# Attention with four PSUM banks for the scores and three for the exponents, and the exponential taken one unit at a time

## The chip, the core and the metric

The kernel runs on one core of a Trainium2 chip. The metric is the device time of one execution in microseconds (us). Five engines work side by side, each through its own instructions in order: PE (TensorE, matrix products; its weight loads are listed apart as PEld), DVE (VectorE), ACT (ScalarE), POOL (GpSimd) and SP (SyncE, which here only issues transfers). They wait for each other through semaphores. PE writes its products into PSUM, of which the kernel has eight banks of 512 fp32 columns.

## The reference

One transformer layer over 8 sequences of 512 tokens and 256 features: attention with 16 heads of 16 features and a bias by relative position, then a mixture of experts, both added to the input.

```
q, k, v = (layernorm(x) @ W.T, split into heads)
scores = einsum('bhqd,bhkd->bhqk', q, k) * SCALING + position_bias
attn = softmax(scores); ctx = einsum('bhqk,bhkd->bhqd', attn, v)
x = x + ctx @ Wo.T
x = x + shared expert + top-2 of 7 routed experts (layernorm(x))
```

## The kernel before

The program has three parts: `project` (q, k, v and the bias tables), `attend` (the attention up to the context) and `finish` (output projection and experts). The change lies in `attend` alone.

`attend` works through 32 items (NI): 4 groups of heads times 8 sequences, each with 4 heads. An item has 8 steps (STEPS). A step is one pair of heads and one block of 128 positions, and has two units, side 0 and side 1, one for each head of the pair. The two sides sit in the two halves of PE's rows (partitions 0 and up, and 64 and up), so that a matmul of side 0 and one of side 1 can run at the same time. Each unit is 128 x 512 numbers, one PSUM bank.

Every unit is computed twice, in two orientations. `scores` (L731) makes q.k for 128 queries by 512 keys in a bank of pS; DVE (`maxima`, L680) adds the bias and takes the row's maximum. `turn` (L684) and POOL's transfers bring the maxima of an item back, as rows of q_st, into the second orientation. `exponents` (L743) makes k.q minus the maximum for 128 keys by 512 queries in a bank of pE: one matmul per side (L757) and then eight narrow ones (L765) that add the bias in a band, alternating between side 0 and side 1. ACT takes the exponential into prob (L711). `values` (L770) multiplies prob by v into pC, and ACT copies pC out once an item (L719).

The order on PE is written out by hand: each turn of `slot` (L783) has `scores` for the step 15 steps ahead (LEAD), `exponents` for the present step, and after every second step `values` for a part of the item before. Two steps with one `values` are called a pair below; the first of its steps is step A, the second step B. The first item has no `values` in its turns. The last 15 steps have no `scores`. The first 15 steps' scores are made ahead, before the first turn.

The waits that the change touches, with their lines:

- pS has three banks. BANK and PLACES (L557, L558) deal units out to them and `held` (L560) gives the unit whose maximum must have been taken before the bank is written again. In plain words a unit waits for the one three places before it (L739). In step B, side 1 has to wait for side 0 of step A.
- pE has four banks, two per step. A step waits once, in front of both sides, for the exponentials of the step two before it (L753). Its last band matmul raises e_mm once (L768), and ACT takes both banks in one instruction of 1024 columns (L711).

Of the kernel before, what the change touches and what calls it, by code (L numbers as in the profile page):

```python
# [525 lines left out]
def attend(nc, mk, g):  # L526
# [8 lines left out]
    with ExitStack() as ctx:  # L535
# [5 lines left out]
        nparts = sb("nparts", [P, KM, HPG, TT], F32R)  # L541
        turned = sb("turned", [P, 2, KM * HPG * TT], F32)
        den_ld, den_inv = sem("den_loaded"), sem("den_inverted")
        pS = ps("pS", [P, 3, S], F32)
        pE = ps("pE", [P, 4, S], F32)
        pC = ps("pC", [P, S], F32)
        s_mm, max_done, split_done, max_turned, max_out, max_ld = (sem(n) for n in (
            "s_mm", "max_done", "split_done", "max_turned", "max_out", "max_loaded"))
# [5 lines left out]
        STEPS = HPG // 2 * TT  # L554
        LEAD = 7

        PLACES = [*range(6), None, *range(6, 14), None, 14, 15]  # L557
        BANK = {unit: k % 3 for k, unit in enumerate(PLACES)}  # L558

        def held(unit):  # L560

            k = PLACES.index(unit) - 3
            while PLACES[k] is None:
                k -= 3
            return PLACES[k] + 1 - (16 if k < 0 else 0)

        def await_stores(engine):

# [4 lines left out]
        with nc.Block() as block:  # L573
            @block.sync
            def _(sp):
                for j in range(HPG):
                    if j == 1:
                        await_stores(sp)
                        loads["step"](sp, 0, 1, True)
                    loads["band"](sp, 0, j)  # L580
                for r in range(2, RING):
                    loads["step"](sp, 0, r, True)

                def store_ctx(quad, r, par):

                    sp.dma_start(ctx_dram[4 * (quad % 2) + r, quad // 2], ctx_sb[:, par]).then_inc(c_out[par], 16)

                def slot(s, u, quad):
                    hg = quad // 2
                    if s >= 2:  # L590
                        sp.wait_ge(evac, s - 1)
                        store_ctx((s - 2) // 4, (u + 2) % 4, u % 2)
                    if quad % 2 == 0 and hg < HG - 1:
                        if hg >= 1:
                            sp.wait_ge(max_done, MAX0 + 16 * 8 * hg)
                            sp.wait_ge(e_mm, STEPS * 8 * hg)
                        loads["near"](sp, hg + 1, u)
                        loads["band"](sp, hg + 1, u)
                    if quad < QUADS - 1:
                        sp.wait_ge(e_mm, STEPS * s + STEPS)  # L600
                        sp.wait_ge(v_ready, s + 1)
                        loads["step"](sp, quad + 1, u, quad % 2 == 1)

                for quad in range(QUADS - 1):
                    for u in range(4):
                        slot(4 * quad + u, u, quad)

                sp.dma_start(g["wo_f"][:], g["woT"].rearrange("(c p) o -> p c o", p=P)).then_inc(g["small_ld"], 16)
                sp.dma_start(g["ga_f"][:], g["gateT"].rearrange("(c p) e -> p c e", p=P)).then_inc(g["small_ld"], 16)
                sp.dma_start(g["eb"][:], g["expert_bias"].rearrange("(e o) -> e o", o=1)).then_inc(g["small_ld"], 16)  # L610
                sp.dma_start(g["b1s"][:], g["b1"]).then_inc(g["small_ld"], 16)
                sp.dma_start(g["b2f"][:], g["b2"]).then_inc(g["small_ld"], 16)
                sp.dma_start(g["b2_low"][:], g["low_rows"]).then_inc(g["small_ld"], 16)
                for par in range(2):
                    sp.dma_start(g["x1"][:, par], g["x_t"][par]).then_inc(g["x_ld"][par], 16)
                for k in range(WS):
                    load_weights(sp, g, k)
                for u in range(4):
                    slot(NI - 4 + u, u, QUADS - 1)
                    if u == 1:  # L620
                        for par in range(2):
                            wait_apart(sp, passed, c_out[par], 16 * (NI // 2 - 2))
                        sp.dma_start(den[:], den_rows(ctx_dram, 2 * DH * S, DW, 0, DH * S)).then_inc(den_ld, 16)
                    if u == 3:
                        wait_apart(sp, passed, den_inv, 1)
                        sp.dma_start(den_rows(rden_dram, S, DW, 0), den[:]).then_inc(rden_out, 16)
                        wait_apart(sp, passed, rden_out, 16)
                        load_context(sp, g, 0)
                for n in (NI - 2, NI - 1):
                    wait_apart(sp, passed, evac, n + 1)  # L630
                    store_ctx(QUADS - 1, n % 4, n % 2)
# [33 lines left out]
            def _(dve):  # L665
                dve.sem_inc(max_done, MAX0)  # L666

                def maxima(m, step):

                    hg = m // 8  # L670
                    pair, t = divmod(step, TT)
                    for side in range(2):
                        j, r = 2 * pair + side, 2 * step + side
                        if m % 8 == 0 and t == 0:
                            dve.wait_ge(near_ld[j], 16 * (hg + 1))
                        unit = 16 * m + r
                        dve.wait_ge(s_mm, unit + 1)
                        dve.wait_ge(max_done, MAX0 + unit - 3)
                        lead = P * t
                        dve.tensor_tensor_reduce(sums[:, r % 4], pS[:, BANK[r]], near[:, hg % 2, j, lead:lead + S], -1.0, BIG,  # L680
                                                 ALU.add, ALU.min,
                                                 nmax[:, j, t:t + 1]).then_inc(max_done, 1)

# [19 lines left out]
            @block.scalar  # L703
            def _(act):
                def slot(n):
                    par = n % 2
                    for step in range(STEPS):
                        if step == 0 and n >= 2:
                            copy_ctx(n - 2)
                        act.wait_ge(e_mm, STEPS * n + step + 1)  # L710
                        act.activation(prob[:, par, 2 * step:2 * step + 2], pE[:, 2 * (step % 2):2 * (step % 2) + 2],  # L711
                                       ACT.Exp).then_inc(exp_done, 1)

                def copy_ctx(n):
                    par = n % 2
                    act.wait_ge(pv_done, PV0 + 4 * n + 4)
                    if n >= 2:
                        act.wait_ge(c_out[par], 16 * (n // 2))
                    act.activation(ctx_sb[:, par], pC[:, ORDER[0]], ACT.Copy).then_inc(evac, 1)  # L719

                for n in range(NI):
                    slot(n)
                copy_ctx(NI - 2)
                copy_ctx(NI - 1)

            @block.tensor
            def _(pe):
# [3 lines left out]
                def scores(m, r, rounds, step):  # L731

                    pair, t = divmod(step, TT)
                    if step == 0:
                        pe.wait_ge(qk_ld[r], 16 * 8 * rounds)
                    for side in range(2):
                        unit = 2 * step + side
                        rows = slice(HALF * side, HALF * side + KQ)
                        pe.wait_ge(max_done, MAX0 + 16 * m + held(unit))  # L739
                        pe.matmul(pS[:, BANK[unit]], q_st[rows, r, pair, P * t:P * t + P], k_st[rows, r, pair],  # L740
                                  start=True, stop=True).then_inc(s_mm, 1)

                def exponents(n, r, step, quad, u, first):  # L743
# [5 lines left out]
                    if step == 0:  # L749
                        pe.wait_ge(far_ld[r], 32 * (quad // 2 + 1))  # L750
                        pe.wait_ge(max_ld, 32 * (n + 1))
                    if not (first and step < 2):
                        pe.wait_ge(exp_done, STEPS * n + step - 1)  # L753
                    bank = 2 * (step % 2)
                    for side in range(2):
                        rows = slice(HALF * side, HALF * side + KS)
                        pe.matmul(pE[:, bank + side], k_st[rows, r, pair, P * t:P * t + P], q_st[rows, r, pair],  # L757
                                  start=True, stop=False, skip_group_check=True)
                    for half in range(2):
                        a, z = band(2 * t + half)  # L760
                        lead = a - band_start(2 * t + half)
                        for part in range(2):
                            for side in range(2):
                                rows = slice(HALF * side, HALF * side + HALF)
                                ins = pe.matmul(pE[:, bank + side, a:z], place[rows, half],  # L765
                                                bandT[rows, (quad // 2) % 2, pair, part, lead:lead + z - a],
                                                start=False, stop=half == 1 and part == 1, skip_group_check=True)
                    ins.then_inc(e_mm, 1)  # L768

                def values(n, par, t, first=False):  # L770

                    if t == 0:
                        pe.wait_ge(exp_done, STEPS * n + STEPS)
                        pe.wait_ge(v_ready, n + 1)
                        if not first:
                            pe.wait_ge(evac, n)
# [510 lines left out]
```

## Time and profile before

| | |
|---|---|
| median of 3 runs | 1020.58 us (1019.04 to 1022.09) |
| the profiled execution | 1021.6 us, its span 1019.8 us |
| PE busy | 966.6 us, 95% of the span |
| DVE busy | 703.4 us, 69% |
| ACT busy | 514.8 us, 50% |
| POOL busy | 109.4 us, 11% |
| exponential, L711, 256 instructions of 1024 columns | 261.3 us, 1025 ns each |
| maxima, L680, 512 instructions of 512 columns | 324.8 us, 686 ns each |

The span is the time between the first and the last instruction of the program; the profiled execution's own time also has what lies around it. A busy PE is not a PE at its peak: matmuls overlap, their ends are modelled, and an engine that is held up in the middle of a stretch of matmuls can still be listed as busy. For PE, the distance between the starts of two instructions tells more than their lengths.

### The profile page before, as it was taken

How to read it: one execution, taken by the hardware profiler on the slowest of the kernel's cores; microseconds unless marked ns; L12 is line 12 of the kernel's file. 1: busy time of each engine (PE TensorE's matmuls, PEld its weight loads, DVE VectorE, ACT ScalarE, POOL GpSimd, SP SyncE). 2: the span in 40 equal slices, each digit the busy share in tenths (PEclk: the TensorE clock that was granted, in tenths of full speed). 3: DMA queues.
4: the chain of work that ended last, by engine and by line, in shares of the span. 5: the costliest groups of instructions: out<-in, count | busy, mean ns of one | idle time of the engine just before them, and what ended most of it. 6: DMA issues, size and time to landing. Idle time of an engine off the chain costs nothing. (4 is left out here: it accounts for less than half of the span.)

```text
span 1019.8 us, 20280 instructions
## 1 busy us (share of the span) xinstructions
PE 966.6 (95%) x7264; PEld 721.1 (71%) x7264; DVE 703.4 (69%) x2048; ACT 514.8 (50%) x680; POOL 109.4 (11%) x245
## 2 busy tenths in 40 slices
PE   5799599999999999999999499999999999999998
PEld 3688266666666666666665388888888798888887
DVE  5575587777787877777781667666666575766664
ACT  2344046666666666666667355444344334434433
POOL 2111021111111111111111100000000000000000
PEclk9899589999999999999999699999999999999999
DMA  4998864334543444333352411101111110101000
GB/s 115 303 342 282 240 136 125 104 95 120 132 115 105 125 136 127 86 94 93 87 156 80 134 42 52 60 25 43 41 42 43 41 41 21 62 1 42 1 22 21
DMA packets 65715, 100.27 MB, mean 98 GB/s; under 512 B 11256, under 2 KB 39440, under 8 KB 65598
## 3 DMA queue, kind: packets, MB, share of 16 engines
q1 hardware_dynamic: 62386, 97.49, 31.8%
q0 software_dynamic: 3072, 1.11, 1.0%
q8 instruction: 51, 0.84, 0.4%
q10 hardware_dynamic: 172, 0.56, 0.2%
q14 instruction: 34, 0.28, 0.1%
HBM read 63.67 MB, written 34.93 MB: 97 GB/s over the span
## 5 line engine op out<-in xcount | busy, mean ns | idle before, releaser
L680 DVE CUSTOM_DVE_ANT_0 sums<-pS,near 128x512 bf16<-128x512 f32 x512 | 324.8, 686 | 91.0 <-PE pS L740 90.7
L711 ACT ACTIVATE prob<-pE 128x1024 f32<-128x1024 f32 x256 | 261.3, 1025 | 173.4 <-PE pE L765 173.0
L1187 PE MATMUL pD<-w2p,h_p 128*128 128x256 f32 x1536 | 203.0, 285 | 1.8 <-DVE x L1037 1.8
L1187 PEld LDWEIGHTS pD<-w2p,h_p 128*128 128x128 f32 x1536 | 191.4, 188 | 11.2 <-DVE x L1037 2.6
L765 PEld LDWEIGHTS pE<-bandT,place 64*128 64x128 f32 x2048 | 183.6, 188 | 16.4
L1169 PE MATMUL pU<-x2T,w1p 128*128 128x512 f32 x768 | 191.7, 399 | 0.0
L1100 ACT ACTIVATE h_f<-pU,b1s 128x512 f32<-128x512 f32 x128 | 88.1, 688 | 191.8 <-PE pU L1169 185.9
L740 PE MATMUL pS<-k_st,q_st 48*128 48x512 f32 x512 | 171.8, 493 | 11.5 <-DVEq L666 7.7
L765 PE MATMUL pE<-bandT,place 64*128 64x244 f32 (+2 forms) x2048 | 181.8, 270 | 0.0
L740 PEld LDWEIGHTS pS<-k_st,q_st 48*128 48x128 f32 x512 | 75.3, 191 | 142.3 <-DVE nmax L680 132.3
L1169 PEld LDWEIGHTS pU<-x2T,w1p 128*128 128x128 f32 x768 | 141.6, 190 | 29.5
L1037 DVE SCALAR_TENSOR_TENSOR x<-pD,combine,x 128x256 f32<-128x256 f32 x256 | 110.8, 478 | 64.0 <-PE pD L1187 62.4
L757 PE MATMUL pE<-q_st,k_st 62*128 62x512 f32 x512 | 142.6, 423 | 0.0
L779 PE MATMUL pC<-prob,v_aug 128*32 128x512 f32 x1024 | 135.7, 604 | 1.0 <-ACT ctx_sb L719 1.0
L1026 DVE TENSOR_TENSOR h_p<-h_f,h_p 128x512 fp32r<-128x512 f32 x128 | 86.8, 690 | 68.0 <-ACT h_p L1103 65.6
L1103 ACT ACTIVATE h_p<-pU,b1s 128x512 fp32r<-128x512 f32 x128 | 87.2, 681 | 0.0
L757 PEld LDWEIGHTS pE<-q_st,k_st 62*128 62x128 f32 x512 | 61.4, 187 | 6.2 <-ACT prob L711 5.0
L472 PE MATMUL pQ<-xT,w_p 128*128 128x512 f32 x192 | 51.3, 420 | 7.8 <-DVE qk L390 5.8
L472 PEld LDWEIGHTS pQ<-xT,w_p 128*128 128x128 f32 x192 | 37.4, 203 | 19.6 <-DVE qk L390 9.9
L214 POOL TENSOR_SCALAR rtmp<-mv 128x4 f32<-128x4 f32 x16 | 5.8, 364 | 422.8 <-DVE mv L946 359.1
L649 POOL DMA_DIRECT2D q_st<-negated_maxima x64 | 34.8, 548 | 83.5 <-DMA negated_maxima<-turned 83.5
L680 DVE DVE_READ_ACCUMULATOR2_ANT nmax<- 128x1 f32 x512 | 42.4, 83 | 0.0
(102 smaller groups left out, 575.4 us busy)
## 6 DMA issues: line engine op xcount, KB each, us to landing
x<-in_x SPq DMA_DIRECT2D x16, 512.0 KB, 4.4
q_parts<-qk SPq DMA_DIRECT2D x16, 512.0 KB, 5.0
k_parts<-qk SPq DMA_DIRECT2D x16, 512.0 KB, 4.6
q_st<-q_parts SPq DMA_DIRECT2D x64, 128.0 KB, 2.8
k_st<-k_parts SPq DMA_DIRECT2D x64, 128.0 KB, 2.9
ctx<-ctx_sb SPq DMA_DIRECT2D x32, 256.0 KB, 2.7
near<-bias_by_distance SPq DMA_DIRECT2D x16, 448.0 KB, 5.7
v_rows<-vs SPq DMA_DIRECT2D x8, 512.0 KB, 3.4
```

The lines of the kernel that those rows point to most:

```text
L472: ins = pe.matmul(pQ[:, m % 2], w_p[:, a, w, c, P * h:P * h + P], xT[:, par, z, c], start=k == 0, stop=k == 5)
L680: dve.tensor_tensor_reduce(sums[:, r % 4], pS[:, BANK[r]], near[:, hg % 2, j, lead:lead + S], -1.0, BIG, ALU.add, ALU.min, nmax[:, j, t:t ...
L711: act.activation(prob[:, par, 2 * step:2 * step + 2], pE[:, 2 * (step % 2):2 * (step % 2) + 2], ACT.Exp).then_inc(exp_done, 1)
L740: pe.matmul(pS[:, BANK[unit]], q_st[rows, r, pair, P * t:P * t + P], k_st[rows, r, pair], start=True, stop=True).then_inc(s_mm, 1)
L757: pe.matmul(pE[:, bank + side], k_st[rows, r, pair, P * t:P * t + P], q_st[rows, r, pair], start=True, stop=False, skip_group_check=True)
L765: ins = pe.matmul(pE[:, bank + side, a:z], place[rows, half], bandT[rows, (quad // 2) % 2, pair, part, lead:lead + z - a], start=False, st ...
L779: ins = pe.matmul(pC[32 * j:32 * j + 32], v_aug[:, par, t, j], prob[:, par, at], start=t == 0, stop=t == TT - 1, skip_group_check=True)
L1037: dve.scalar_tensor_tensor(out=row, in0=pD[:, t // 2, t % 2], scalar=combine[:, par, t, e:e + 1], in1=row, op0=ALU.mult, op1=ALU.add).then ...
L1100: act.activation(h_f[:, e % 2, m], pU[:, e % 2, m], ACT.Gelu, bias=b1s[:, e, m:m + 1])
L1103: act.activation(h_p[:, e % 2, 0, m], pU[:, e % 2, m], ACT.Gelu, bias=b1s[:, e, m:m + 1]).then_inc(s["h_hi"], 1)
L1169: ins = pe.matmul(pU[:, e % 2, m], w1p[:, e, a, c, P * m:P * m + P], x2T[:, par, c, z], start=k == 0, stop=k == 5)
L1187: ins = pe.matmul(pD[:, t2, u], h_p[:, e % 2, a, m, P * t:P * t + P], w2p[:, e, z, m], start=k == 0 and e < NE - 1, stop=k == 5)
```

## The change

pS gets a fourth bank and pE gives one up. Units now go round robin: unit number modulo 4 for pS, modulo 3 for pE, with units counted over all items. PLACES, BANK and `held` go. Each unit of scores waits for the maximum of the unit four before it. In `exponents` each side has a wait of its own, for the exponential of the unit three before it; the wait of side 1 stands between the two matmuls of L757. The last band matmul of each side raises e_mm, so it counts units and not steps, and ACT takes the exponential of 512 columns, one unit at a time. Other waits on e_mm and exp_done are scaled to match.

```diff
-        pS = ps("pS", [P, 3, S], F32)
-        pE = ps("pE", [P, 4, S], F32)
+        pS = ps("pS", [P, 4, S], F32)
+        pE = ps("pE", [P, 3, S], F32)
...
+        PS, PX = 4, 3
...
-                        act.wait_ge(e_mm, STEPS * n + step + 1)
-                        act.activation(prob[:, par, 2 * step:2 * step + 2], pE[:, 2 * (step % 2):2 * (step % 2) + 2],
-                                       ACT.Exp).then_inc(exp_done, 1)
+                        for side in range(2):
+                            unit = 16 * n + 2 * step + side
+                            act.wait_ge(e_mm, unit + 1)
+                            act.activation(prob[:, par, 2 * step + side], pE[:, unit % PX], ACT.Exp).then_inc(exp_done, 1)
...
-                        unit = 2 * step + side
+                        unit = 16 * m + 2 * step + side
                         rows = slice(HALF * side, HALF * side + KQ)
-                        pe.wait_ge(max_done, MAX0 + 16 * m + held(unit))
-                        pe.matmul(pS[:, BANK[unit]], q_st[rows, r, pair, P * t:P * t + P], k_st[rows, r, pair],
+                        pe.wait_ge(max_done, MAX0 + unit + 1 - PS)
+                        pe.matmul(pS[:, unit % PS], q_st[rows, r, pair, P * t:P * t + P], k_st[rows, r, pair],
...
-                    if not (first and step < 2):
-                        pe.wait_ge(exp_done, STEPS * n + step - 1)
-                    bank = 2 * (step % 2)
+                    bank = [(16 * n + 2 * step + side) % PX for side in range(2)]
                     for side in range(2):
                         rows = slice(HALF * side, HALF * side + KS)
-                        pe.matmul(pE[:, bank + side], k_st[rows, r, pair, P * t:P * t + P], q_st[rows, r, pair],
+                        if 16 * n + 2 * step + side >= PX:
+                            pe.wait_ge(exp_done, 16 * n + 2 * step + side + 1 - PX)
+                        pe.matmul(pE[:, bank[side]], k_st[rows, r, pair, P * t:P * t + P], q_st[rows, r, pair],
                                   start=True, stop=False, skip_group_check=True)
...
-                    ins.then_inc(e_mm, 1)
+                                if half == 1 and part == 1:
+                                    ins.then_inc(e_mm, 1)
```

On PE, a pair in the middle of the second item, from before. Names in brackets are the semaphores on which an instruction waits (max_done is raised by DVE, exp_done by ACT):

```order
L740 MATMUL pS<-k_st,q_st 128x512 [waits max_done] x2
L757 MATMUL pE<-q_st,k_st 128x512 [waits exp_done]
L757 MATMUL pE<-q_st,k_st 128x512
L765 MATMUL pE<-bandT,place 128x244 x8
L740 MATMUL pS<-k_st,q_st 128x512 [waits max_done] x2
L757 MATMUL pE<-q_st,k_st 128x512 [waits exp_done]
L757 MATMUL pE<-q_st,k_st 128x512
L765 MATMUL pE<-bandT,place 128x218 x4
L765 MATMUL pE<-bandT,place 128x154 x4
```

And the same pair of the changed kernel, with the `values` that follow it:

```order
L733 MATMUL pS<-k_st,q_st 128x512 [waits max_done] x2
L750 MATMUL pE<-q_st,k_st 128x512 [waits exp_done] x2
L758 MATMUL pE<-bandT,place 128x244 x8
L733 MATMUL pS<-k_st,q_st 128x512 [waits max_done] x2
L750 MATMUL pE<-q_st,k_st 128x512 [waits exp_done] x2
L758 MATMUL pE<-bandT,place 128x218 x4
L758 MATMUL pE<-bandT,place 128x154 x4
L773 MATMUL pC<-prob,v_aug 32x512 x4
```

The matmuls and their order are the same; what moved is the second wait on exp_done, which now stands on side 1's matmul, in front of all band matmuls of the step.

On ACT, the first items, from before and then of the changed kernel:

```order
L711 ACTIVATE prob<-pE 128x1024 [waits e_mm] x16
L719 ACTIVATE ctx_sb<-pC 128x512 [waits pv_done]
L711 ACTIVATE prob<-pE 128x1024 [waits e_mm] x8
L719 ACTIVATE ctx_sb<-pC 128x512 [waits pv_done]
L711 ACTIVATE prob<-pE 128x1024 [waits e_mm] x8
```

```order
L705 ACTIVATE prob<-pE 128x512 [waits e_mm] x32
L712 ACTIVATE ctx_sb<-pC 128x512 [waits pv_done]
L705 ACTIVATE prob<-pE 128x512 [waits e_mm] x16
L712 ACTIVATE ctx_sb<-pC 128x512 [waits pv_done]
L705 ACTIVATE prob<-pE 128x512 [waits e_mm] x16
```

Each exponential of 1024 columns became two of 512 with a wait each; the copies of the context stand where they stood.

## Rows read from the trace of the kernel before

**Rows 1.** Windows: busy time by engine, clock; columns are stretch, PE, PEld, DVE, ACT, POOL.
```profile
111.00:134.00 23.00, 18.95 (x35) 8.46 (x37) 20.25 (x66) 0.00 (x0) 3.40 (x6) 0.50 0.89 195
134.00:144.00 10.00, 9.80 (x94) 8.47 (x90) 8.99 (x30) 7.06 (x7) 2.19 (x4) 0.85 0.43 95
144.00:537.00 393.00, 392.80 (x3724) 246.08 (x3724) 311.14 (x1020) 256.08 (x263) 63.07 (x116) 1.00 0.41 114
537.00:556.00 19.00, 19.00 (x216) 11.52 (x218) 3.19 (x8) 14.87 (x16) 2.17 (x4) 1.00 0.23 79
```

**Rows 2.** Waits between 144 and 537 us: total, times, longest.
```profile
ACT prob L711 <- PE pE L765: 136.6, 231, 1.2
PEld pS L740 <- DVE nmax L680: 118.9, 232, 0.8
```

**Rows 3.** Timeline of PE, one pair: start, length, instruction.
```profile
401.05 0.50 PE L740 MATMUL pS<-k_st,q_st 48*128 48x512 f32 x2
401.39 0.40 PE L757 MATMUL pE<-q_st,k_st 62*128 62x512 f32 x2
401.63 0.60 PE L765 MATMUL pE<-bandT,place 64*128 64x154 f32 x8
402.06 0.77 PE L740 MATMUL pS<-k_st,q_st 48*128 48x512 f32 x2
...
403.45 1.06 PE L779 MATMUL pC<-prob,v_aug 128*32 128x512 f32 x8
```

**Rows 4.** Timeline of PE's weight loads around the wait in that pair.
```profile
402.34 0.18 PEld L740 LDWEIGHTS pS<-k_st,q_st 48*128 48x128 f32 x1 [0.19 <-DVE nmax L680]
402.35 0.29 PEld L757 LDWEIGHTS pE<-q_st,k_st 62*128 62x128 f32 x2
```

**Rows 5.** Timeline of ACT in that pair and the next one.
```profile
401.19 0.60 ACT L719 ACTIVATE ctx_sb<-pC 128x512 f32<-128x512 f32 x1
402.27 1.03 ACT L711 ACTIVATE prob<-pE 128x1024 f32<-128x1024 f32 x1 [0.48 <-PE pE L765]
...
405.69 1.03 ACT L711 ACTIVATE prob<-pE 128x1024 f32<-128x1024 f32 x1 [1.11 <-PE pE L765]
```

**Rows 6.** Timeline of DVE in the same pair.
```profile
401.59 0.69 DVE L680 CUSTOM_DVE_ANT_0 sums<-pS,near 128x512 bf16<-128x512 f32 x1 [0.82 <-PE pS L740]
402.20 0.08 DVE L680 DVE_READ_ACCUMULATOR2_ANT nmax<- 128x1 f32 x1
```

**Rows 7.** Timeline of PE, start and values of the pair after it.
```profile
404.45 0.51 PE L740 MATMUL pS<-k_st,q_st 48*128 48x512 f32 x2
...
406.81 1.07 PE L779 MATMUL pC<-prob,v_aug 128*32 128x512 f32 x8
```

**Rows 8.** Timeline of PE and ACT where no scores are left.
```profile
542.49 0.62 PE L765 MATMUL pE<-bandT,place 64*128 64x244 f32 x8
...
543.04 1.06 PE L779 MATMUL pC<-prob,v_aug 128*32 128x512 f32 x8
...
544.04 0.50 PE L757 MATMUL pE<-q_st,k_st 62*128 62x512 f32 x2
...
545.03 1.94 ACT L711 ACTIVATE prob<-pE 128x1024 f32<-128x1024 f32 x2 [0.64 <-PE pE L765]
545.06 0.57 PE L765 MATMUL pE<-bandT,place 64*128 64x218 f32 x8
...
545.56 1.07 PE L779 MATMUL pC<-prob,v_aug 128*32 128x512 f32 x8
```

**Rows 9.** Timeline of DVE in the scores made ahead.
```profile
116.58 0.69 DVE L680 CUSTOM_DVE_ANT_0 sums<-pS,near 128x512 bf16<-128x512 f32 x1 [0.27 <-PE pS L740]
```

**Rows 10.** The page, part 5: the other ACT operation of 512 columns.
```profile
L1100 ACT ACTIVATE h_f<-pU,b1s 128x512 f32<-128x512 f32 x128 | 88.1, 688 | 191.8 <-PE pU L1169 185.9
```

**Rows 11.** Timeline of ACT and PE at the end of the stage.
```profile
557.01 0.60 ACT L719 ACTIVATE ctx_sb<-pC 128x512 f32<-128x512 f32 x1
...
557.73 0.19 PEld L779 LDWEIGHTS pC<-prob,v_aug 128*32 128x32 f32 x8 [1.86 <-ACT prob L711]
```

More of the change, by code:

```diff
@@ L555, in attend @@
         LEAD = 7
[L557 to L565, printed above, removed]
+        PS, PX = 4, 3
         def await_stores(engine):
@@ L595, in slot @@
                             sp.wait_ge(max_done, MAX0 + 16 * 8 * hg)
-                            sp.wait_ge(e_mm, STEPS * 8 * hg)
+                            sp.wait_ge(e_mm, 16 * 8 * hg)
                         loads["near"](sp, hg + 1, u)
@@ L599, in slot @@
                     if quad < QUADS - 1:
-                        sp.wait_ge(e_mm, STEPS * s + STEPS)
+                        sp.wait_ge(e_mm, 16 * s + 16)
                         sp.wait_ge(v_ready, s + 1)
@@ L679, in maxima @@
                         lead = P * t
-                        dve.tensor_tensor_reduce(sums[:, r % 4], pS[:, BANK[r]], near[:, hg % 2, j, lead:lead + S], -1.0, BIG,
+                        dve.tensor_tensor_reduce(sums[:, r % 4], pS[:, unit % PS], near[:, hg % 2, j, lead:lead + S], -1.0, BIG,
                                                  ALU.add, ALU.min,
@@ L764, in exponents @@
                                 rows = slice(HALF * side, HALF * side + HALF)
-                                ins = pe.matmul(pE[:, bank + side, a:z], place[rows, half],
+                                ins = pe.matmul(pE[:, bank[side], a:z], place[rows, half],
                                                 bandT[rows, (quad // 2) % 2, pair, part, lead:lead + z - a],
                                                 start=False, stop=half == 1 and part == 1, skip_group_check=True)
-                    ins.then_inc(e_mm, 1)
+                                if half == 1 and part == 1:
+                                    ins.then_inc(e_mm, 1)
                 def values(n, par, t, first=False):
                     if t == 0:
-                        pe.wait_ge(exp_done, STEPS * n + STEPS)
+                        pe.wait_ge(exp_done, 16 * n + 16)
                         pe.wait_ge(v_ready, n + 1)
```

## The prediction

> **What bounds the kernel now.** I read the windows first, then the waits, then the timeline of one pair of steps engine by engine, since the first two only say where to look. In the windows the attention from 144 to 537 us has PE busy for 392.80 of 393 us, while DVE has 311.14 and ACT 256.08 [rows 1]. A reader is to see two things: PE leads this stage, and a busy share of 100% cannot tell whether it is held up inside. The waits can. ACT waits for PE's band matmuls 231 times, 136.6 us in all, so it is far from the bound; the weight loads of the scores wait for DVE's maxima 232 times, 118.9 us, which is twice a pair [rows 2]. The 3724 matmuls of that window at 32 a pair (4 of L740, 4 of L757, 16 of L765, 8 of L779, as the trace counts them) are 116.4 pairs, so a pair takes 393 / 116.4 = 3.38 us.
>
> The timeline of one pair says which of the two waits costs something. Step A starts at 401.05, its L757 at 401.39, its bands at 401.63, step B at 402.06, and the values at 403.45; the next pair starts at 404.45 [rows 3, 7]. So step A takes 1.01, step B 1.39 and the values 1.00 us. The wait at the start of a pair costs nothing: PE is still busy with the values before it. The one in step B does cost. Side 0 of the scores starts at 402.06, side 1 has its weights only at 402.34, after a wait for DVE [rows 3, 4]. What holds it is the three banks: side 1 of B needs the maximum of side 0 of A, which DVE starts at 401.59 and has at 402.20 + 0.08 = 402.28 [rows 6]; PE goes on 0.06 later. That gives the price of a hand-over to PE, 0.06 us. The rows also show that PE passes nothing by a wait: L757's weights come at 402.35, right behind the waiting load, though their banks had long been free [rows 4]. I lean on that below.
>
> **The fourth bank of scores.** Side 1 of B now needs side 1's partner two steps back, in the pair before, so its wait ends long before it is asked. Without the wait, step B would run as a matmul of 512 columns does when PE is warm, 401.63 - 401.39 = 0.24 us each for the scores and for L757 [rows 3], and then the bands up to the values, 543.04 - 542.49 = 0.55 us for the wide ones and 545.56 - 545.06 = 0.50 us for the narrow ones [rows 8]. The values would start at 1.01 + 0.24 + 0.24 + 0.55 = 2.04 us after the pair's start, where they now start at 2.40 [rows 3]; in the next pair at about 2.02 where they now start at 406.81 - 404.45 = 2.36 [rows 7]. So up to 0.35 us a pair is there to be won, 41 us over 116 pairs.
>
> **The third bank of exponents.** With three banks, side 1 of a step needs the exponential of side 0 of the step right before it; before, both sides needed only the step before that. This is the same short loop as the one taken away from the scores, with ACT in DVE's place, and it starts later in the step. Side 0's last band matmul stands next to side 1's, so its exponential starts when the exponential of step A starts now: 402.27 - 401.05 = 1.22 us after the pair's start [rows 3, 5], in the next pair 405.69 - 404.45 = 1.24 [rows 5, 7]. No exponential of 512 columns is in the trace. The nearest is ACT's copy of 512 columns out of PSUM, 0.60 us [rows 5], and the Gelu of 512 columns takes 0.69 [rows 10]. I take 0.60, since the exponential of 1024 columns at 1.03 [rows 5] is 0.43 more than the copy for 512 columns more, as it would be if both follow one line; 0.69 is the upper end. Add 0.06 for the hand-over (upper end 557.73 - 557.61 = 0.12, from ACT's copy to the loads of the values [rows 11]). Side 1 of L757 in step B is then let go at 1.22 + 0.60 + 0.06 = 1.88 us. Undisturbed it would go at 1.01 + 0.24 = 1.25 or a little later. Everything behind it waits too: eight band matmuls, the values, and the next pair. From the release a cold start costs 401.39 - 401.05 = 0.34 us up to the first band [rows 3], and the bands 0.55, so the values start at 1.88 + 0.34 + 0.55 = 2.77, against 2.40 now: 0.37 us more. For the next pair 1.90 + 0.34 + 0.50 = 2.74 against 2.36: 0.38 more. The lost 0.35 of the scores is already in these, since the old wait is no longer part of the path. Over 116 pairs: 116 x 0.375 = 43.5 us. A pair becomes about 3.75 us.
>
> In step A the new wait costs nothing: its side 1 needs side 0 of the B before it, whose exponential is done during the 1.00 us of values plus 0.34. The split on ACT itself costs nothing either. Four exponentials at 0.60 and a quarter of a copy make 2.55 us in a pair of 3.75; what hides them is PE. If that cover were gone it would show as ACT busy all through, and it is not near.
>
> **Where no scores are left** nothing stands between the steps to cover ACT. These are the last 8 pairs (216 matmuls at 28 a pair is 7.7 [rows 1]; the first of the 8 has scores in its step A alone). A pair starts at 544.04, its first exponential at 545.03, its values at 545.56 [rows 8], so 0.99 and 1.52 us in. After the change the release comes at 0.99 + 0.66 = 1.65, the values at 1.65 + 0.34 + 0.50 = 2.49: 0.97 more, 8 x 0.97 = 7.8 us.
>
> **The first item** has no values to cover ACT, so each of its steps waits on the last. From a release 0.34 to the bands, 402.27 - 401.63 = 0.64 from there to the exponential [rows 3, 5], 0.66 for it: 1.64 us a step, or 1.53 if side 0, whose tile is free while side 1 waits, runs ahead by one of the four rounds of bands, (402.06 - 401.63) / 4 = 0.11 [rows 3]. Now a step takes 10 us / (94 / 12) = 1.28 [rows 1]. Seven steps at +0.25 to +0.36: I take +2.
>
> **The scores made ahead**, from 111 to 134 us, are DVE's: 20.25 of 23 us busy [rows 1]. Now and then it waits for a bank's matmul, 0.27 us at a time [rows 9]; a fourth bank takes away perhaps four of those: -1.
>
> **Sum.** 43.5 + 7.8 + 2 - 1 = +52. The profiled execution took 1021.6 us (span 1019.8), which gives 1074; it lies 1.0 above the median of the runs, so 1073. The ends of the unknowns: an exponential of 0.69 adds 0.09 x 124 = 11; a hand-over of 0.12 adds 7; if the start after the release is as warm as between two matmuls (0.24 for 0.34), 12 come off.
>
> What a separate increment of e_mm for each side may cost is not in the sum, because the rows show none: the scores' pair carries two increments and DVE starts at 401.59, 0.04 after its end at 401.55 [rows 3, 6]; the bands carry one, and ACT starts at 402.27, 0.04 after their end at 402.23 [rows 3, 5]. The Trainium skill (TensorE: Matmul & The Clock Gate, "The cost: per-tile semaphore tail") says that increments on neighbouring tiles of the array are carried out one after the other, some 26 ns for each. By that rule one more increment a step, at the worst on the path to the exponential of step A, would be an estimated 0.026 x 124 = 3 us more.
>
> **Rivals.**
> - The exponential of one unit comes in time (faster). ACT starts a unit without the other and is through in half the time, so the loop of 0.66 us could be shorter than I think, and the fourth bank's 41 us would be kept: 1021 - 41 - 1 = 979 us. It decides at one place, side 1 of L757 in step B: its release would have to come by 1.25 us after the pair's start to win all, and by 1.88 - 0.37 = 1.51 to lose nothing. For it speaks that ACT has 136.6 us of waits [rows 2]. Against it: the exponential cannot start before 1.22, and 0.03 to 0.29 us is less than any ACT instruction of 512 columns takes here [rows 5, 10]. 4 in 100. Between the two, no change: 2 in 100.
> - The wait is real but half as dear, because PE works off side 0's bands while side 1 waits. That would need matmuls to pass a waiting load, which rows 4 deny; the path through side 1 (0.34 + 0.55) would also stay. With half the price, 0.19 x 124 = 24, it gives about 1045. 4 in 100.
> - The clock. The granted clock was 1.00 from 144 to 556 us and 0.50 from 111 to 134, where PE had 35 matmuls in 23 us [rows 1]. The change puts a stop of about half a us into every pair and a longer one into each of the last 8. Should the clock fall to its lower level, 1.2 GHz, for a tenth of the stage, the parts of a pair that are PE's own (1.01 + 0.89 + 1.00 = 2.90 us) would take about twice as long there: 12 pairs x 2.9 = 35 us more, 1108. Against it, PE still has work in 2.9 of 3.75 us. The Trainium skill (TensorE: Matmul & The Clock Gate, "A second HAM failure mode: psum-queue depth-cycling") tells of a kernel in which PE paused briefly between groups while it went round the PSUM banks, and the clock kept going down and up; the trace before shows the pauses in step B at an unbroken 1.00, which speaks against it here. 4 in 100.
> - The forecast has the remaining 86 in 100.
>
> **How the numbers follow.** Runs of this kernel differ by some 0.3%, and I take that as the least that can be told from no change. The forecast, the half price and the clock make it slower: 0.94. Faster 0.04, same 0.02. Time 1073 us. For the range the forecast's own unknowns give 1061 to 1091 at their ends; both upper ends together are unlikely. I take 1057 to 1088.
>
> **What would show it.** In the waits, the entry of L740's loads for DVE in step B goes; only the harmless one at a pair's start stays. A new one appears, PE's loads of the exponents' matmuls for ACT's exponential, once a pair (about 0.5 us each) and twice in the first item. Step A keeps 1.01 us, step B goes from 1.39 to about 1.76, the values stay at 1.00, a pair is 3.75. The exponential is 0.60 us, and ACT's busy time rises to some 512 x 0.60 = 307 us for it. The stage after 560 us is only shifted. I am wrong if side 1 of step B is let go before 1.5 us into the pair, if the wait falls on another instruction, or if the granted clock in the attention falls below 1.00.

## The result, and where the time went

| | before | changed |
|---|---|---|
| median | 1021.11 us (1019.04 to 1022.09, 4 runs) | 1071.57 us (1070.60 to 1074.86, 4 runs) |
| span of the profiled execution | 1019.8 us | 1068.8 us |

The ratio is 1.050, with a 95% interval of 1.047 to 1.053. The forecast was 1073 us.

I cut both traces at the same events: on PE the first exponents' matmul, the first `values`, the `values` 115 pairs later and the last scores, and then the first instruction of `finish`. Between the 115 pairs and the last scores lies 1.0 us in both, which the table leaves out. Differences are taken before rounding.

| stage | before | changed | difference |
|---|---|---|---|
| up to the first exponents' matmul | 133.4 | 132.9 | -0.5 |
| from there to the first `values` (the first item) | 13.4 | 18.8 | +5.3 |
| 115 pairs | 3.377 each | 3.716 each | +39.0 |
| from the last scores to `finish` | 26.7 | 34.1 | +7.4 |
| `finish` | 456.9 | 454.7 | -2.2 |

These add up to +49.0, as much as the spans differ. The last line is not the change's: nothing in `finish` was touched, and among the kernels below it takes 454.7 to 457.9 us.

The waits of the changed kernel from 144 to 557 us (engine, line, releaser: total, times, longest):

```profile
ACT prob L705 <- PE pE L758: 154.2, 223, 1.1
DVE sums L672 <- PE pS L733: 112.3, 111, 1.3
PEld pS L733 <- DVE nmax L672: 91.4, 109, 0.8
PEld pE L750 <- ACT prob L705: 73.2, 113, 0.7
...
PE pE L750 <- ACT prob L705: 23.7, 111, 0.3
```

This window holds 111 pairs; that of [rows 2] held 116, with 232 waits of the scores' loads for DVE, two a pair. Now these loads (L733) wait 109 times, once a pair: the wait inside the pair is gone, the one at its start (under the `values` of the pair before) stays. In its place the loads of the exponents' matmuls (now L750) wait for ACT, once a pair, 0.65 us each. ACT itself waits more than before, 1.39 us a pair (154.2 / 111) against 1.18 (136.6 / 116). It is not short of time; it is asked too late.

One pair on PE (start, length, instruction), the counterpart of [rows 3, 7]:

```profile
405.36 0.49 PE L733 MATMUL pS<-k_st,q_st 48*128 48x512 f32 x2
405.69 0.40 PE L750 MATMUL pE<-q_st,k_st 62*128 62x512 f32 x2
405.93 0.62 PE L758 MATMUL pE<-bandT,place 64*128 64x244 f32 x8
406.38 0.39 PE L733 MATMUL pS<-k_st,q_st 48*128 48x512 f32 x2
406.61 0.39 PE L750 MATMUL pE<-q_st,k_st 62*128 62x512 f32 x1
407.23 0.50 PE L750 MATMUL pE<-q_st,k_st 62*128 62x512 f32 x1 [0.23 <-ACT prob L705]
407.23 0.90 PE L758 MATMUL pE<-bandT,place 64*128 64x218 f32 x8
408.06 1.06 PE L773 MATMUL pC<-prob,v_aug 128*32 128x512 f32 x8
409.06 0.50 PE L733 MATMUL pS<-k_st,q_st 48*128 48x512 f32 x2
```

ACT in the same pair, and the weight load that waits for it:

```profile
406.58 1.09 ACT L705 ACTIVATE prob<-pE 128x512 f32<-128x512 f32 x2 [1.13 <-PE pE L758]
```
```profile
407.22 0.18 PEld L750 LDWEIGHTS pE<-q_st,k_st 62*128 62x128 f32 x1 [0.65 <-ACT prob L705]
```

Both scores of step B start together at 406.38, where in [rows 3, 4] the second was held up. Then side 0 of L750 goes at 406.61 and side 1 only at 407.23. The exponential starts 1.22 us into the pair, and 0.64 later side 1's load goes: an exponential of 0.59 and a hand-over of 0.05. Note that PE counts as busy to the very start of its [0.23] of idle time: the hole is 0.6 us wide in the starts and 0.2 in the busy time.

### The profile page after: what moved, and what is told of

The parts are those of the page before. It is cut to its first block and busy times, and to the rows that moved or that the text cites. A ratio compares the mean times of both kernels' runs of the same rounds, so it can differ in the third digit from the quotient of the medians.

```text
span 1068.8 us, 20536 instructions
## 1 busy us (share of the span) xinstructions
PE 987.9 (92%) x7264; PEld 715.1 (67%) x7264; DVE 703.4 (66%) x2048; ACT 531.8 (50%) x936; POOL 109.4 (10%) x245
## 5 line engine op out<-in xcount | busy, mean ns | idle before, releaser
L705 ACT ACTIVATE prob<-pE 128x512 f32<-128x512 f32 x512 | 278.0, 594 | 206.1 <-PE pE L758 206.1
L758 PE MATMUL pE<-bandT,place 64*128 64x244 f32 (+2 forms) x2048 | 202.0, 280 | 0.0
L750 PE MATMUL pE<-q_st,k_st 62*128 62x512 f32 x512 | 170.9, 431 | 29.7 <-ACT prob L705 28.5
L1163 PE MATMUL pU<-x2T,w1p 128*128 128x512 f32 x768 | 189.5, 396 | 0.0
L758 PEld LDWEIGHTS pE<-bandT,place 64*128 64x128 f32 x2048 | 178.1, 190 | 10.6
L733 PE MATMUL pS<-k_st,q_st 48*128 48x512 f32 x512 | 130.4, 473 | 10.3 <-DVEq L658 7.8
L750 PEld LDWEIGHTS pE<-q_st,k_st 62*128 62x128 f32 x512 | 74.1, 189 | 93.2 <-ACT prob L705 90.9
L733 PEld LDWEIGHTS pS<-k_st,q_st 48*128 48x128 f32 x512 | 56.6, 195 | 116.9 <-DVE nmax L672 106.7
```

The lines of the kernel that those rows point to most:

```text
L705: act.activation(prob[:, par, 2 * step + side], pE[:, unit % PX], ACT.Exp).then_inc(exp_done, 1)
L733: pe.matmul(pS[:, unit % PS], q_st[rows, r, pair, P * t:P * t + P], k_st[rows, r, pair], start=True, stop=True).then_inc(s_mm, 1)
L750: pe.matmul(pE[:, bank[side]], k_st[rows, r, pair, P * t:P * t + P], q_st[rows, r, pair], start=True, stop=False, skip_group_check=True)
L758: ins = pe.matmul(pE[:, bank[side], a:z], place[rows, half], bandT[rows, (quad // 2) % 2, pair, part, lead:lead + z - a], start=False, sto ...
L1163: ins = pe.matmul(pU[:, e % 2, m], w1p[:, e, a, c, P * m:P * m + P], x2T[:, par, c, z], start=k == 0, stop=k == 5)
```

## The experiments

All times are medians. Each ratio is to runs of the kernel before taken beside that kernel (their medians are 1020.5 to 1021.1 us). A pair and the two stages are read from one trace of each kernel, the pair as above. "First item" is the time from the first exponents' matmul to the first `values`, "last part" from the last scores to `finish`.

| kernel | time, us | ratio to before (95%) | pair | first item | last part |
|---|---|---|---|---|---|
| before | 1021.1 | | 3.377 | 13.4 | 26.7 |
| changed | 1071.6 | 1.050 (1.047 to 1.053) | 3.716 | 18.8 | 34.1 |
| split_only | 1021.2 | 1.000 (0.998 to 1.001) | 3.378 | 13.5 | 26.8 |
| rr3 | 1020.2 | 0.999 (0.998 to 1.000) | 3.377 | 13.4 | 26.7 |
| rr3_swap | 987.2 | 0.966 (0.964 to 0.968) | 3.067 | 18.7 | 26.7 |
| after_swap | 1100.0 | 1.076 (1.074 to 1.078) | 3.972 | 20.3 | 34.1 |
| before_halfmax | 988.5 | 0.968 (0.967 to 0.970) | 3.110 | 12.8 | 26.7 |
| after_halfmax | 1066.7 | 1.047 (1.044 to 1.051) | 3.718 | 16.5 | 34.1 |
| after_halfexp | 1041.3 | 1.021 (1.019 to 1.024) | 3.505 | 14.7 | 32.4 |
| after_side0_first | 1068.0 | 1.046 (1.044 to 1.048) | 3.716 | 14.4 | 34.1 |
| swap_late | 984.0 | 0.964 (0.962 to 0.965) | 3.066 | 13.3 | 26.7 |

### The two harmless parts

split_only is the changed kernel with the banks as before (PLACES, BANK and `held` are back for pS):

```diff
-        pS = ps("pS", [P, 4, S], F32)
-        pE = ps("pE", [P, 3, S], F32)
+        pS = ps("pS", [P, 3, S], F32)
+        pE = ps("pE", [P, 4, S], F32)
...
-        PS, PX = 4, 3
+        PX = 4
```

> The kernel before with one part of the change: the exponential taken one unit of 512 columns at a time, with a wait for each side, but four banks of exponents and three of scores as before. My theory: with four banks side 1 of a step needs the exponential of side 1 two steps back, which is long done, so nothing stalls: 1021 us (1018 to 1024), a pair of steps 3.38 us, no wait of L757's loads for ACT. Rival, the split itself costs (ACT's fixed cost twice, two increments a step): at least 3 us more, and 1070 if the split were the whole cause.

Measured 1021.2 us, 3.378 us a pair. Taking the exponential one unit at a time, with its 512 instructions, its waits and its increments, costs nothing that can be measured.

rr3 is the kernel before with round robin over its three banks of scores (DVE reads the bank `unit % PS` too):

```diff
+        PS = 3
...
-                        unit = 2 * step + side
+                        unit = 16 * m + 2 * step + side
...
-                        pe.wait_ge(max_done, MAX0 + 16 * m + held(unit))
-                        pe.matmul(pS[:, BANK[unit]], q_st[rows, r, pair, P * t:P * t + P], k_st[rows, r, pair],
+                        pe.wait_ge(max_done, MAX0 + unit + 1 - PS)
+                        pe.matmul(pS[:, unit % PS], q_st[rows, r, pair, P * t:P * t + P], k_st[rows, r, pair],
```

> The kernel before with the other small part: the units of scores go round robin over the three banks (unit number modulo 3, counted over all items) instead of by the table PLACES. My theory: in step B side 1 still waits for side 0 of step A, so 1021 us (1018 to 1024) and a pair of 3.38 us. Rival, the table was worth something: some us slower.

Measured 1020.2 us, 3.377 a pair: the table was worth nothing that can be measured against round robin. So the whole loss sits in the number of banks.

### What side 1 waits for

after_halfexp is the changed kernel with half of each exponential left out. ACT fills the columns left out once, before the first item:

```diff
-                            act.activation(prob[:, par, 2 * step + side], pE[:, unit % PX], ACT.Exp).then_inc(exp_done, 1)
+                            act.activation(prob[:, par, 2 * step + side, 0:S // 2], pE[:, unit % PX, 0:S // 2], ACT.Exp).then_inc(exp_done, 1)
...
+                act.wait_ge(near_ld[0], 16)
+                act.wait_ge(s_mm, 17)
+                for k in range(2 * HPG * TT):
+                    act.activation(prob[:, k // 16, k % 16, S // 2:S], near[:, 0, 0, 0:S // 2], ACT.Exp)
```

> The changed kernel with the exponential taken over the first 256 of a unit's 512 columns (the other half of the exponentials is left out; ACT fills those columns of prob once, before the first item). My theory: what PE waits for in step B is side 0's exponential of step A, nearly all of it its own length. From 1025 ns at 1024 columns and 594 at 512 it should be about 380 ns at 256, so the release comes 0.21 us earlier: a pair falls from 3.71 to 3.50, 115 x 0.21 = 24 us, the last 8 pairs 2, the first item 1 to 2: 1044 us (1036 to 1052). Rival, the hand-overs PE to ACT to PE are the cost and not the length: less than 5 us.

Measured 1041.3 us. The exponential's line on the page of the changed kernel, and of this one:

```profile
L705 ACT ACTIVATE prob<-pE 128x512 f32<-128x512 f32 x512 | 278.0, 594 | 206.1 <-PE pE L758 206.1
```
```profile
L705 ACT ACTIVATE prob<-pE 128x256 f32<-128x256 f32 x512 | 168.5, 381 | 242.4 <-PE pE L762 242.4
```

The instruction is 0.213 us shorter, and a pair is 3.716 - 3.505 = 0.211 shorter; the last part loses 1.7 us over its 8 pairs, again 0.21 each. What is taken off that one exponential comes off the pair in full. The first item is another 4.1 us shorter, where the clock was up from 137 us on (in the changed kernel from 148). That ACT is 50% idle does not help it.

after_halfmax is the changed kernel with half of each maximum left out; before_halfmax leaves out the same in the kernel before:

```diff
-                        dve.tensor_tensor_reduce(sums[:, r % 4], pS[:, unit % PS], near[:, hg % 2, j, lead:lead + S], -1.0, BIG,
+                        dve.tensor_tensor_reduce(sums[:, r % 4, 0:S // 2], pS[:, unit % PS, 0:S // 2], near[:, hg % 2, j, lead:lead + S // 2], -1.0, BIG,
```

> The changed kernel with the same half of the maxima left out. My theory: with four banks DVE is off the path in every pair, so nothing is gained there (3.71 us a pair stays); the scores made ahead, DVE's before, may give 3 us: 1068 us (1063 to 1073). Rival, DVE still holds PE in the changed kernel: 20 us or more gained.

> The kernel before, with DVE's maximum taken over the first 256 of a unit's 512 columns (the other half of the work of the maxima is left out). My theory: the price of the three banks of scores is DVE's time between side 0 of step A and side 1 of step B. DVE's instruction falls from 0.69 to some 0.47 us and its spacing from 0.61 to 0.40; side 1 of B is released before it is asked for, a pair falls from 3.38 to 3.05 to 3.07 us, 115 pairs give 36 us, the scores made ahead some 3 more: 982 us (974 to 990). Rival, PE is at its own limit in step B and DVE's wait is only listed: less than 6 us gained, all of it in the scores made ahead.

In the changed kernel the pair stays at 3.718, so DVE is off the path there. The medians differ by 4.9 us; in the two traces the first exponents' matmul comes 2.4 us earlier and the first item is 2.3 us shorter, mostly since its clock rose earlier (see the windows of both below). In the kernel before, the pair falls to 3.110 and the time by 32 us, to 988.5, inside the stated range, though 6 more than the number I gave. A pair of it on PE:

```profile
401.18 0.50 PE L740 MATMUL pS<-k_st,q_st 48*128 48x512 f32 x2
401.52 0.40 PE L757 MATMUL pE<-q_st,k_st 62*128 62x512 f32 x2
401.75 0.62 PE L765 MATMUL pE<-bandT,place 64*128 64x244 f32 x8
402.21 0.50 PE L740 MATMUL pS<-k_st,q_st 48*128 48x512 f32 x2
402.45 0.48 PE L757 MATMUL pE<-q_st,k_st 62*128 62x512 f32 x2
402.69 0.67 PE L765 MATMUL pE<-bandT,place 64*128 64x218 f32 x8
403.28 1.06 PE L779 MATMUL pC<-prob,v_aug 128*32 128x512 f32 x8
```

Step B runs at 0.24 us a matmul as in a pair with no wait. Its scores still take 0.50 and not 0.39 us as in the changed kernel, and the bands to `values` 0.59 where [rows 8] have 0.50. A trace of the wait for DVE is left:

```profile
402.07 0.08 DVE L680 DVE_READ_ACCUMULATOR2_ANT nmax<- 128x1 f32 x1
402.11 0.28 PEld L740 LDWEIGHTS pS<-k_st,q_st 48*128 48x128 f32 x2
```

The maximum of side 0 of step A is done at 402.15. The first of the two loads goes at 402.11; the second ends at 402.39 and lasts 0.18, so it goes at 402.21: some 0.05 behind the maximum, which is the price of a hand-over, and 0.10 behind the first.

### Which work lies inside the loop

after_side0_first is the changed kernel, but in step B side 0's four bands are issued before side 1's matmul and its wait:

```diff
...
+                    if step % 2 == 1:
+                        for side in range(2):
+                            main(side)
+                            for half, part in four:
+                                near_band(side, half, part)
+                    else:
+                        for side in range(2):
+                            main(side)
+                        for half, part in four:
                             for side in range(2):
...
+                                near_band(side, half, part)
```

Here main(side) is the wait and the matmul of L750, near_band one band matmul with its increment.

> The changed kernel, but in odd steps (step B) PE gets side 0's matmul and its four bands first, and only then side 1's matmul with its wait, and its four bands. PE then has work to issue while it waits. My theory: the path runs through side 1 alone (release, its matmul, its four bands, values), so nothing is gained in a pair: 1071 us (1065 to 1076); in the first item side 0's exponential of step B is ready earlier, which may give 1 to 3 us. Rival, half the price is that side 0's bands stand behind the wait: 1045 to 1055.

Measured 1068.0 us. The pair is 3.716 us to the last digit, and the last part too is unchanged:

```profile
402.30 0.39 PE L751 MATMUL pE<-q_st,k_st 62*128 62x512 f32 x1
402.53 0.57 PE L758 MATMUL pE<-bandT,place 64*128 64x218 f32 x4
402.91 0.50 PE L751 MATMUL pE<-q_st,k_st 62*128 62x512 f32 x1
403.25 0.57 PE L758 MATMUL pE<-bandT,place 64*128 64x218 f32 x4
403.75 1.06 PE L786 MATMUL pC<-prob,v_aug 128*32 128x512 f32 x8
```

Side 0's bands now run at 402.53, in the hole. It is filled and not shorter: side 1 starts at 402.91, 1.87 us into the pair that began at 401.04. The rival of half the price falls. The medians differ by 3.6 us, and what is gained is in the first item, 4.3 us in the traces.

rr3_swap and after_swap change one thing in either kernel, the order in step B:

```diff
+                        if step % 2 == 1:
+                            exponents(n, u, step, quad, u, first and u == 0)
                         if not (last and u + ahead > 3):
                             scores(n + ahead, (u + ahead) % 4, quad + 1 + (u + ahead) // 4, other)
-                        exponents(n, u, step, quad, u, first and u == 0)
+                        if step % 2 == 0:
+                            exponents(n, u, step, quad, u, first and u == 0)
```

> As rr3, and in odd steps (step B) the exponents' matmuls come before the scores' and not after them. Banks stay at three for scores and four for exponents. My theory: the loss in step B was the short loop scores of A, maximum by DVE, scores of B; with L757 and the bands of B in between, side 1's bank is free before it is asked for. A pair takes about 3.04 us (0.34 less), 116 pairs give 39 us: 981 us (975 to 992), and L740's waits for DVE inside a pair go. Rival, the number of banks is what counts and the order is not: 1021.

> The changed kernel (four banks for scores, three for exponents) with the same swap in odd steps. My theory: here the short loop runs over the exponents, and the scores of step B were the only work between the bands of A and side 1 of L757 in B. ACT's release stays at about 1.85 us after the pair's start; the scores now come behind it, 0.26 us more in front of the values: a pair of about 3.97 us, 116 x 0.26 = 30 us more, 1101 us (1090 to 1110). Rival, the stall is not a matter of what covers ACT: 1072.

Both lie in their ranges, 987.2 and 1100.0 us (after_swap 1 below its number, rr3_swap 6 above: the pairs took 3.067 and not 3.04 us, which makes 3 us, and the rest lies in the first item, 18.7 us for 13.4 in the trace). The same edit gains 33 us with three banks of scores and four of exponents (against rr3), and costs 28 us with four and three. PE in rr3_swap, one pair:

```profile
400.04 0.50 PE L732 MATMUL pS<-k_st,q_st 48*128 48x512 f32 x2
400.38 0.40 PE L749 MATMUL pE<-q_st,k_st 62*128 62x512 f32 x2
400.61 0.60 PE L757 MATMUL pE<-bandT,place 64*128 64x154 f32 x8
401.05 0.40 PE L749 MATMUL pE<-q_st,k_st 62*128 62x512 f32 x2
401.29 0.61 PE L757 MATMUL pE<-bandT,place 64*128 64x244 f32 x8
401.74 0.39 PE L732 MATMUL pS<-k_st,q_st 48*128 48x512 f32 x2
402.06 1.06 PE L771 MATMUL pC<-prob,v_aug 128*32 128x512 f32 x8
```

The scores of step B are asked for 1.70 us into the pair, both sides at once; in [rows 3, 4] side 1 was let go at 1.29. After_swap has the same order and this step B:

```profile
404.39 0.40 PE L750 MATMUL pE<-q_st,k_st 62*128 62x512 f32 x1
405.24 0.49 PE L750 MATMUL pE<-q_st,k_st 62*128 62x512 f32 x1 [0.45 <-ACT prob L705]
405.24 0.71 PE L758 MATMUL pE<-bandT,place 64*128 64x218 f32 x6
405.75 0.43 PE L733 MATMUL pS<-k_st,q_st 48*128 48x512 f32 x1
405.79 0.35 PE L758 MATMUL pE<-bandT,place 64*128 64x154 f32 x2
405.98 0.43 PE L733 MATMUL pS<-k_st,q_st 48*128 48x512 f32 x1
406.34 1.07 PE L773 MATMUL pC<-prob,v_aug 128*32 128x512 f32 x8
```

Its pair began at 403.37, so side 1 is again let go at 1.87; the hole is 0.85 us wide, since the scores that had covered 0.24 of it now stand behind it.

### The first item, and a version that beats both

swap_late is rr3_swap with the old order in the first item (`step % 2 == 1 and n > 0` in the edit above).

> As rr3_swap (three banks of scores, four of exponents, exponents before scores in step B), but the first item keeps the old order. In rr3_swap the time from the first exponents to the first values was 18.7 us at a granted clock of 0.50, against 13.5 us in the kernel before, where the clock was up to 1.00 for most of it. My theory: the old order keeps PE busier in the first item, the clock rises as it did before, and those 5 us come back while the pairs stay at 3.07 us: 982 us (979 to 986). Rival, the clock of the first item does not follow from its order: 987.

Measured 984.0 us. The clock during the first item (PEclk is the first of the last three numbers), before, changed and swap_late, in stretches of 4 us:

```profile
134.00:138.00 4.00, 4.00 (x37) 3.60 (x33) 3.04 (x12) 2.20 (x3) 0.69 (x1) 0.64 0.94 216
138.00:142.00 4.00, 3.80 (x38) 3.11 (x37) 3.95 (x13) 2.96 (x4) 1.50 (x3) 1.00 0.11 19
```
```profile
134.00:138.00 4.00, 3.96 (x25) 2.92 (x25) 2.57 (x8) 2.17 (x4) 0.69 (x1) 0.50 0.83 203
138.00:142.00 4.00, 3.95 (x27) 2.97 (x24) 2.40 (x9) 2.17 (x4) 1.49 (x3) 0.50 0.03 7
142.00:146.00 4.00, 3.94 (x25) 2.92 (x24) 2.47 (x9) 2.09 (x4) 0.00 (x0) 0.50 0.02 4
```
```profile
134.00:138.00 4.00, 4.00 (x34) 3.71 (x32) 3.26 (x12) 2.05 (x2) 0.70 (x1) 0.50 0.75 211
138.00:142.00 4.00, 3.97 (x43) 3.30 (x41) 3.60 (x13) 3.10 (x4) 1.50 (x3) 0.89 0.29 45
```

In the changed kernel and in rr3_swap PE begins some 25 matmuls in 4 us and stays at 0.50, 1.2 GHz, past 146 us (0.79 and 0.72 are their means from 146 to 150). In the kernel before and in swap_late it begins 34 to 37 from 134 to 138 us, and is at 1.00 from about 137 and 139 us on, as the means 0.64 and 0.89 say. With the changed kernel's order the clock can rise as early, as after_halfmax shows:

```profile
134.00:138.00 4.00, 3.91 (x29) 2.76 (x27) 1.68 (x9) 2.32 (x5) 1.50 (x3) 0.64 0.70 175
138.00:142.00 4.00, 3.02 (x32) 2.18 (x32) 2.32 (x12) 3.11 (x6) 0.00 (x0) 1.00 0.47 124
```

The clock also differs between runs of one kernel. One of the four runs of after_halfmax took 1073.8 us at a mean clock of 0.964 over its span, the other three 1066.4 to 1066.9 us at 0.973 to 0.975. The trace of rr3_swap is of the slowest of its four runs (mean clock 0.964); the fastest took 984.6 us at 0.971, and the runs of swap_late have 0.968 to 0.972. So these traces show what the late clock costs. That the order of the first item decides when the clock rises is not shown. The stages of swap_late are those forecast: pairs of 3.066 us and a first item of 13.3 us instead of 18.7. On the whole time, the two intervals (0.964 to 0.968 for rr3_swap, 0.962 to 0.965 for swap_late) overlap, so the 3 us between them are shown by the stage in the two traces and not by the runs. Against the runs of the kernel before beside it, swap_late gains 36 us (1020.5 - 984.0), against the changed kernel 88.

## Why the prediction was right

- **The removed wait** went as forecast. It had been put at up to 0.35 us a pair. The swap, which leaves no wait inside most pairs, brings a pair to 3.067, 0.31 less; half maxima, which leave a trace of the wait, to 3.110, 0.27 less.
- **The new wait** was the main step, and each of its terms can be laid beside its measurement: start of the exponential 1.22 and 1.24 us after the pair's start (1.21 and 1.22 as means over the pairs of either kind), its length 0.60 (0.594), hand-over 0.06 (0.05), release at 1.88 and 1.90 (1.86 and 1.87), from there to the `values` 0.89 and 0.84 (0.88 and 0.84; 408.06 - 407.22 in the pair shown). Together 0.375 us a pair, measured 3.716 - 3.377 = 0.339. The 0.036 between them is small pieces: the release came 0.02 to 0.03 earlier than forecast, and the way from it to the `values` was 0.01 shorter.
- **That PE passes nothing by a waiting load**, on which the forecast leaned, held: side 0's bands, whose bank was free, follow side 1's load at 407.23, and moving them ahead of it (after_side0_first) changed no pair.
- **The cover of step A** held: no wait for ACT at a pair's start, and half an exponential changes a pair by one length and not two.
- **The last 8 pairs**: +7.8 forecast, +7.4 measured, 0.92 us each. **The scores made ahead**: -1 forecast, -0.5 measured.
- **The first item** was mis-sized: +2 forecast, +5.3 measured. The mechanism, each step waiting on the last, was right, but its terms (0.34, 0.64 and 0.66 us) were read at a clock of 1.00, and the clock did not rise until 147.7 us (the mean of 0.79 from 146 to 150). From one side 0 of L750 to the next, the five steps from 136.60 to 147.09 us take 2.10 each at 0.50. The next two take 1.46 and 1.49, and in after_halfmax, where the clock was up from 136.9 us (the 0.64 from 134 to 138), the five from 137.79 to 145.36 take 1.51. The forecast had 1.53 to 1.64. Five steps at 0.59 more are 3.0 of the 3.3 us missed: that part is the clock's.
- **The rivals.** In the pairs the clock stayed at 1.00, as the forecast had it. The Trainium skill (TensorE: Matmul & The Clock Gate, "A second HAM failure mode: psum-queue depth-cycling") tells of a clock that went down and up where PE paused briefly between groups; pauses of 0.6 us in every 3.7 brought no such fall here. The rival of an exponential in time would have needed a release by 1.51 us; it came at 1.86. The rival of half the price is refuted by after_side0_first.
- **The extra increments**: the exponential of step A starts 1.22 us into a pair with wide bands in its step A (405.36 to 406.58), against 1.24 in the like pair of [rows 5, 7]. The estimate by the Trainium skill (TensorE: Matmul & The Clock Gate, "The cost: per-tile semaphore tail"), 0.026 us a step on the path, is not borne out, nor by split_only.

That the total came within 2 us of the forecast is partly luck: the first item's miss (+3.3) and the pairs' (39.0 for 43.5, so -4.5) have opposite signs, and `finish`, which the change did not touch, was 2.2 us shorter in this trace. What makes the clock rise late in the first item is left open.

## What to carry over

Here a bank given from the exponents to the scores did not remove the wait; it chose which of the two loops is short. Write down, for each bank, how far back the reader is whose release it needs and what work of the writing engine lies in between, and price it by the reader's single-instruction latency, not by its busy share. If the loop is a little too short, moving work of the same engine into it (here the scores behind the exponents in every second step, 36 us) may do what another bank was meant to.

## What I had not expected of the hardware

- ACT's exponential out of PSUM takes 381, 594 and 1025 ns for 256, 512 and 1024 columns: 0.83 to 0.84 ns a column and about 165 ns besides. The Trainium skill (ScalarE: Activation LUTs, "Step-by-step: what each stage is for") gives 0.833 ns an element, which agrees. Two in a row overlap: the pair of 512 takes 1.09 us, less than two times 0.594.
- Where no load waits, PE can begin matmuls out of the program's order: in after_swap a matmul of the scores starts at 405.75 while two band matmuls, which stand before it in the program, start from 405.79 on. It looks as if each half of PE's rows keeps its own order and side 0 had run ahead; the rows do not name the side, so this is inferred.
- In the changed kernel's trace the first item stayed at 1.2 GHz for all but its end, and cost 5.3 us where its waits had been priced at 2.
